# Front of a mixture-of-experts block: zero rows leave earlier, GpSimd normalises 20 of 32 tiles, the statistics and the router weights in another order

## Chip, cores and metric

One core of a Trainium2 chip runs the kernel. The metric is the device time of one execution in microseconds (us). The kernel before the change takes 130.73 us, the median of 3 runs (130.49 to 130.87).

## What is computed

The input x holds 16 sequences of 256 tokens, 128 wide: 4096 tokens. The result is x plus the outputs of two branches on the layer-normalised x. One branch is a gated recurrence, the other sends each token to one of 8 experts.

```python
xn = _layernorm(x, axis=-1)
x = x + _L0_attn_ref(xn, ...) + _L0_ffn_ref(xn, ...)

# recurrence: causal depthwise convolution of 4 taps, two gates, scan, projection, RMS norm
r_t = sigmoid(x_conv @ W_r.T + b_r);  i_t = sigmoid(x_conv @ W_i.T + b_i)
a_t = a_base ** (8.0 * r_t)
h = a * h + b                       # over the 256 tokens of a sequence
out = out @ W_out.T * rms * gamma

# experts: E = 8, capacity 512 tokens each
eidx = argmax(softmax(xf @ Wr))
rank = cumulative count of earlier tokens of the same expert;  keep = rank < cap
ye = relu(xf[dispatch] @ W1) @ W2
y  = zeros.at[dispatch].add(ye * probability)
```

## The kernel before

The 4096 tokens are 32 tiles of 128 tokens (NT = 32). They are loaded and normalised in five units, `UNITS = ((0, 4), (4, 4), (8, 8), (16, 8), (24, 8))`, first tile and count. Each of the five engines has one program, written out by hand in the order in which it runs, and engines wait for each other by semaphores. An engine that waits stops everything behind the wait in its program.

The front, which the change touches, runs from the start to the first gather of expert rows:

- SP (sync) issues the five loads of x (L314), then waits for the last of them (L315), then issues the weights of expert 0 (L318). It then issues, for each unit, the write of the normalised rows to the DRAM buffer `xn_rows` (L323) as soon as the unit is normalised, with the weights of expert 1 behind the third. Last come gamma (L326) and four writes of zeros to the result rows `y_rows` (L330).
- DVE takes mean and variance of a unit (`moments(u)`, L874), and after ACT's square root (`root(u)`, L682) the reciprocal and the offset (`inverse(u)`, L882 and L884). The offset releases the normalisation of the unit. It also routes: `marks(h)` (L918 to L934) finds the expert of each token of half h (16 tiles) and counts along a partition, `ranks(h)` (L943 to L947) adds the counts from PE, `places(h)` (L952 to L964) makes the masks `hi_val` and `low_eq`. At the end the table from PE is turned into `idx_in` and `idx_out` (L985, L986).
- POOL (GpSimd) builds constants, writes the numbers `values` (L385, four instructions), normalises its tiles (`POOL_TILES`, L380), and makes the four diagonal matrices of the convolution taps, `diag` (L396), between units 2 and 3. Later it issues the indirect gathers (L405) and scatters (L417).
- ACT evicts the transposed raw tiles (`untile(n)`, L694), normalises its tiles (`ACT_TILES`, L689) and evicts the transposed normalised tiles (`keep_columns(n)`, L698).
- PE starts with 7 matmuls on the identity whose result nobody reads (L442, two passes each). It transposes raw x (L507), makes the centred router weights (L513), computes router logits (L453), and counts over partitions (`counts(h)`, L461 to L473). The order on PE in the middle of the front is fixed by these lines:

```python
for n in range(1, 3):
    columns_of(n)          # L495, transposes of normalised tiles
conv(0, 0, 2)              # L537, L539; waits for diag_done = 4 (L524)
counts(1)                  # L461 to L473; waits for run of marks(1)
...
table_of(0)                # L481
columns_of(3)
conv(0, 2, 3)
table_of(1)                # L481; its result is read by idx_in
```

The first gather waits for all of `xn_rows` to have landed (`xn_out`, L424) and for `idx_in` (L426). After it PE transposes the gathered rows (`turn(0)`, L594) and the expert matmuls begin. POOL issues 64 gathers and scatters from there to the end of the expert stage, and PE has work in all of it.

Of the kernel before, what the change touches and what calls it, by code (L numbers as in the profile page):

```python
# [13 lines left out]
P = 128  # L14
# [4 lines left out]
C = 4  # L19
TC = T // C  # L20
# [26 lines left out]
def rglru_moe_kernel(nc, x, params, gamma, weights, xn_rows, y_rows, out):  # L47
# [3 lines left out]
    def tile_rows(dram, t0, nt):  # L51

        return dram[t0 * P:(t0 + nt) * P, :].rearrange("(g p i) d -> p g (i d)", p=P, i=RUN)

    def runs(buf, t0, nt):
        return buf[:, t0 * D:(t0 + nt) * D].rearrange("p (g w) -> p g w", w=RUN * D)

    def own_rows(dram, t0, nt):

        return dram[0:T, :].rearrange("(p t) d -> p t d", t=NT)[:, t0:t0 + nt, :]  # L60

    def tiles(buf, t0, nt):
        return buf[:, t0 * D:(t0 + nt) * D].rearrange("p (t d) -> p t d", d=D)

    with ExitStack() as ctx:
# [6 lines left out]
        def sem(name):  # L72
            return ctx.enter_context(nc.semaphore(name))
# [70 lines left out]
        zeros = sca[:, 0:TC]  # L144
# [33 lines left out]
        NU = len(UNITS)  # L178

        x_in = [sem(f"x_in{u}") for u in range(NU)]  # L180
# [3 lines left out]
        zeroed = sem("zeroed")  # L184
        zero_out = sem("zero_out")
# [81 lines left out]
        block = ctx.enter_context(nc.Block())  # L267


        POOL_TILES = (2, 3, 6, 7, 10, 11, 14, 15, 18, 19, 22, 23, 26, 27, 30)  # L270
        ACT_TILES = (0, 1, 4, 5, 8, 9, 12, 13, 16, 17, 20, 21, 24, 25, 28, 29, 31)

        COUNT_AT = 6
        PE_CONV = 2
# [1 line left out]
        def normalised(eng, n):  # L276
            for done, mine in ((norm_act, ACT_TILES), (norm_pool, POOL_TILES)):
                count = sum(t < 4 * (n + 1) for t in mine)
                if count:
                    eng.wait_ge(done, count)  # L280
# [30 lines left out]
        @block.sync  # L311
        def _(sp):
            for u, (t0, nt) in enumerate(UNITS):
                sp.dma_start(runs(x_tok, t0, nt), tile_rows(x_rows, t0, nt)).then_inc(x_in[u], 16)  # L314
            sp.wait_ge(x_in[NU - 1], 16)  # L315

            def first_weights(e):
                sp.dma_start(w_raw[:, e, :], weights[:, e * WW:(e + 1) * WW]).then_inc(w_in[e], 16)  # L318

            first_weights(0)  # L320
            for u, (t0, nt) in enumerate(UNITS):
                normalised(sp, (t0 + nt) // 4 - 1)
                sp.dma_start(own_rows(xn_rows, t0, nt), tiles(xn_tok, t0, nt)).then_inc(xn_out, 16)  # L323
                if u == 2:
                    first_weights(1)
            sp.dma_start(gam[:, :], gamma.partition_broadcast(P)).then_inc(gam_in, 16)  # L326

            sp.wait_ge(zeroed, 1)
            for c in range(C):
                sp.dma_start(y_rows[c * TC:(c + 1) * TC, :].rearrange("(p j) d -> p (j d)", p=P),  # L330
                             zeros).then_inc(zero_out, 16)

            for e in range(2, E):
                sp.wait_ge(gather_in[e - 2], 16 * ST)
                sp.dma_start(w_raw[:, e, :], weights[:, e * WW:(e + 1) * WW]).then_inc(w_in[e], 16)

            sp.wait_ge(scattered, 16 * NS)
            for n in range(NH):
                sp.dma_start(tiles(ybuf, 4 * n, 4), own_rows(y_rows, 4 * n, 4)).then_inc(y_in[n], 16)
            for n in range(0, NH, 2):  # L340
                sp.wait_ge(final_done, n + 1)
                sp.dma_start(tile_rows(out_rows, 4 * n, 4), runs(ybuf, 4 * n, 4)).then_inc(stored, 16)
            sp.wait_ge(stored, 16 * NH)

        @block.gpsimd
        def _(pool):
# [28 lines left out]
            def normalise(u):  # L375
                t0, nt = UNITS[u]
                pool.wait_ge(nmr_done, u + 1)
                for t in range(t0, t0 + nt):
                    if t in POOL_TILES:
                        g.tensor_scalar(xn_tok[:, t * D:(t + 1) * D], x_tok[:, t * D:(t + 1) * D], rstd[:, t:t + 1],  # L380
                                        nmr[:, t:t + 1], ALU.mult, ALU.add).then_inc(norm_pool, 1)
# [8 lines left out]
            normalise(0)  # L390
            normalise(1)
            normalise(2)
            pool.wait_ge(par_in, 16)
            pool.wait_ge(ident_done, 1)
            for k in range(TAPS):
                g.tensor_scalar(diag[:, k, :], ident[:, :], par[:, CONV_W + k:CONV_W + k + 1], 0.0, ALU.mult,  # L396
                                ALU.add).then_inc(diag_done, 1)
            normalise(3)
            normalise(4)

            def gather(e):
                if e > 0:
# [35 lines left out]
        def _(pe):  # L438
            mm = nc.tensor.matmul
            pe.wait_ge(ident_done, 1)  # L440
            for _ in range(7):
                mm(bank[7][:, 0:P], ident[:, :], ident[:, :], start=True, stop=True)  # L442


# [227 lines left out]
        def _(act):  # L672
# [4 lines left out]
            def root(u):  # L677
                t0, nt = UNITS[u]
                if u == 0:
                    act.wait_ge(eps_done, 3)  # L680
                act.wait_ge(stat_done, (t0 + nt) // 2)
                a(std[:, t0:t0 + nt], stats[:, t0:t0 + nt, 2], ACT.Sqrt, bias=eps[:, 0:1],  # L682
                  scale=1.0 / D).then_inc(std_done, 1)

            def normalise(n):
                act.wait_ge(nmr_done, 1 + next(u for u, (t0, nt) in enumerate(UNITS) if 4 * n < t0 + nt))
                for t in range(4 * n, 4 * n + 4):
                    if t in ACT_TILES:
                        a(xn_tok[:, t * D:(t + 1) * D], x_tok[:, t * D:(t + 1) * D], ACT.Identity,  # L689
                          scale=rstd[:, t:t + 1], bias=nmr[:, t:t + 1]).then_inc(norm_act, 1)  # L690

            def untile(n):
                act.wait_ge(tp_done, n + 1)
                a(xT[:, n * HT:(n + 1) * HT], tp[n % 2][:, :], ACT.Copy).then_inc(xT_act, 1)  # L694

            def keep_columns(n):
                act.wait_ge(xn_tp, n + 1)
                a(xnT[:, n * HT:(n + 1) * HT].rearrange("d (p i) -> d p i", i=RUN),  # L698
                  xn_bank[n % 3][:, :].rearrange("d (i p) -> d p i", i=RUN), ACT.Copy).then_inc(xnT_done, 1)
# [4 lines left out]
            root(1)  # L704
            normalise(0)
            untile(2)
            normalise(1)
            root(2)
            untile(3)
            normalise(2)  # L710
            untile(4)
            normalise(3)
            root(3)
            untile(5)
            untile(6)
            normalise(4)
            normalise(5)
            root(4)
            untile(7)
            keep_columns(0)  # L720
            normalise(6)
            normalise(7)
            for n in range(1, 4):
                keep_columns(n)

            def lead(e):
# [127 lines left out]
        def _(dve):  # L854
# [14 lines left out]
            def moments(u):  # L869
                t0, nt = UNITS[u]  # L870
                dve.wait_ge(x_in[u], 16)
                for t in range(t0, t0 + nt, 2):

                    v.bn_stats(stats[:, t:t + 2, :].rearrange("p t c -> p (t c)"),  # L874
                               x_tok[:, t * D:(t + 2) * D].rearrange("p (j d) -> p d j", j=2)
                               ).then_inc(stat_done, 1)

            def inverse(u):
                t0, nt = UNITS[u]
                cols = slice(t0, t0 + nt)  # L880
                dve.wait_ge(std_done, u + 1)
                v.reciprocal(rstd[:, cols], std[:, cols]).then_inc(rstd_done, 1)  # L882
                dve.wait_ge(rstd_done, u + 1)
                v.scalar_tensor_tensor(nmr[:, cols], stats[:, cols, 1], -1.0, rstd[:, cols], ALU.mult,  # L884
                                       ALU.mult).then_inc(nmr_done, 1)

            moments(0)
            dve.wait_ge(centre_mm, 1)
            v.tensor_copy(w_router[:, :], centred).then_inc(router_w, 1)
            moments(1)  # L890
            inverse(0)
            inverse(1)
            moments(2)
# [2 lines left out]
            v.tensor_scalar(half_b[:, :], par[:, BIAS_R:BIAS_I + 1], 0.5, None, ALU.mult).then_inc(coef, 1)  # L896
            inverse(2)
            moments(3)
            results = [0]

            def put(ins):
# [64 lines left out]
                                        ALU.is_equal).then_inc(low_done, 1)  # L966

            marks(0)
            inverse(3)
            moments(4)  # L970
            ranks(0)
            inverse(4)
            places(0)
            marks(1)
            ranks(1)
# [129 lines left out]
            def scaled_projection(_):  # L1105
                dve.wait_ge(gam_in, 16)
                v.tensor_tensor(wog[:, :], par[:, WO_T:WO_T + D], gam[:, :], ALU.mult).then_inc(wog_done, 1)
# [97 lines left out]
```

## Time and profile before

| | |
|---|---|
| time, median of 3 runs | 130.73 us |
| span of the profiled execution | 128.8 us |
| PE busy | 106.2 us (82%) |
| DVE busy | 101.8 us (79%) |
| ACT busy | 99.6 us (77%) |
| POOL busy | 84.6 us (66%) |
| chain that ended last, PE's share | 60% |
| moved by DMA | 19.27 MB |

The time of an execution is its span, from the first to the last instruction, and what lies around it: 130.73 less 128.8 is 1.9 us. The page cuts the span into 40 slices of 3.2 us and gives the busy share of each engine in tenths; for the clock, 9 stands for the full rate:

```profile
PE   3999999999799999999999997999997999700000
DVE  5398998999699999979614489999999975973690
ACT  3299792888589589789689999999999799823560
POOL 8987774078788787778777877888787878700000
PEclk9999999999999999999999999999999999998555
```

### The profile page before, as it was taken

The numbers are of one execution on the slowest core, as the hardware profiler recorded it, in microseconds if no ns is written. First come the engines' busy times: TensorE is split into PE (matmuls) and PEld (weight loads), VectorE is DVE, ScalarE is ACT, GpSimd is POOL, SyncE is SP. The second block draws the span as 40 slices with busy tenths as digits, with TensorE's granted clock in tenths as the row PEclk, the third lists the DMA queues.
The fourth block names the chain that finished last, engine by engine and source line by source line (L and its number), as shares of the span: only waits on it lengthen the run. The fifth ranks groups of instructions, "written<-read, shape, count | busy, mean of one in ns | idle before, by whom it ended". The sixth has DMA issues, their size and how long they took to land.

```text
span 128.8 us, 2229 instructions
## 1 busy us (share of the span) xinstructions
PE 106.2 (82%) x711; PEld 89.9 (70%) x711; DVE 101.8 (79%) x238; ACT 99.6 (77%) x219; POOL 84.6 (66%) x109
## 2 busy tenths in 40 slices
PE   3999999999799999999999997999997999700000
PEld 3999976672379779789879987898697899600000
DVE  5398998999699999979614489999999975973690
ACT  3299792888589589789689999999999799823560
POOL 8987774078788787778777877888787878700000
PEclk9999999999999999999999999999999999998555
DMA  2966964892456365312611711111110111149995
GB/s 85 383 247 173 405 244 173 318 380 66 103 169 181 80 209 139 118 53 56 209 41 41 219 51 41 61 37 41 52 57 25 60 43 61 41 108 302 325 372 215
DMA packets 8234, 19.27 MB, mean 150 GB/s; under 512 B 1689, under 2 KB 1945, under 8 KB 8224
## 3 DMA queue, kind: packets, MB, share of 16 engines
q1 hardware_dynamic: 5424, 13.70, 31.5%
q0 software_dynamic: 2080, 4.19, 11.2%
q10 hardware_dynamic: 720, 1.25, 2.6%
q8 instruction: 5, 0.08, 0.2%
q14 instruction: 5, 0.04, 0.1%
HBM read 10.82 MB, written 8.39 MB: 149 GB/s over the span
## 4 chain that ended last, share of the span: by engine, by line
PE 60%; DVE 9%; DMA 8%; ACT 8%; issue 5%; POOL 4%; POOLq 1%; SPq 1%; DVEq 0%; ACTq 0%
PE bank L624 17%; PE bank L609 6%; PE bank L611 6%; PE bank L610 6%; DMA dec<-y_rows 4%; PE bank L640 4%; PE bank L453 3%; PE bank L561 3%; PE bank L442 3%; POOL xn_tok L405 3%; DMA xn_tok<-xn_rows,idx_in 2%; ACT xc L796 2%; PE bank L594 2%; PE bank L563 2%; PE bank L562 2%
## 5 line engine op out<-in xcount | busy, mean ns | idle before, releaser
L405 POOL DMA_INDIRECT xn_tok<-xn_rows,idx_in x32 | 33.7, 1054 | 14.4 <-issue 9.4
L417 POOL DMA_INDIRECT y_rows<-xn_tok,idx_out x32 | 33.5, 1047 | 9.7 <-issue 9.1
L624 PE MATMUL bank<-w_raw,h_sb 128*128 128x128 f32 x256 | 29.9, 275 | 0.0
L624 PEld LDWEIGHTS bank<-w_raw,h_sb 128*128 128x128 f32 x256 | 29.2, 192 | 0.0
L786 ACT ACTIVATE h_sb<-bank 128x512 f32<-128x512 f32 x32 | 18.8, 598 | 2.5 <-PE bank L611 0.6
L609 PE MATMUL bank<-xg_hi,w_hi 128*128 128x512 f32 x32 | 13.2, 412 | 0.0
L611 PE MATMUL bank<-xg_hi,w_lo 128*128 128x512 f32 x32 | 12.6, 393 | 0.0
L610 PE MATMUL bank<-xg_lo,w_hi 128*128 128x512 f32 x32 | 12.5, 391 | 0.0
L1021 DVE SCALAR_TENSOR_TENSOR xc<-xnT,par,xc 128x1020 f32<-128x1020 f32 (+2 forms) x9 | 11.5, 1277 | 0.3
L640 PE MATMUL bank<-par,xc 128*128 128x128 f32 x64 | 8.8, 280 | 2.2 <-ACT xc L796 1.3
L1061 DVE TENSOR_TENSOR_SCAN xnT<-dec,bank 128x256 f32<-128x256 f32 x16 | 10.1, 674 | 0.3
L640 PEld LDWEIGHTS bank<-par,xc 128*128 128x128 f32 x64 | 8.0, 191 | 3.1 <-ACT xc L796 1.6
L805 ACT ACTIVATE sq<-bank 128x128 f32<-128x128 f32 x32 | 8.9, 277 | 1.0 <-PE bank L640 0.3
L836 ACT ACTIVATE dec<-dec,prob 128x128 f32<-128x128 f32 x16 | 5.1, 389 | 5.8 <-DMA dec<-y_rows 5.8
L380 POOL TENSOR_SCALAR xn_tok<-x_tok,rstd,nmr 128x128 f32<-128x128 f32 x15 | 7.7, 529 | 2.8 <-DVE nmr L884 2.8
L453 PE MATMUL bank<-w_router,dec 128*128 128x128 f32 x64 | 8.6, 278 | 0.4 <-ACT dec L694 0.3
L754 ACT ACTIVATE dec<-bank,half_b 128x512 f32<-128x512 f32 x8 | 5.5, 689 | 4.2 <-PE bank L563 3.2
L453 PEld LDWEIGHTS bank<-w_router,dec 128*128 128x128 f32 x64 | 7.8, 192 | 0.9 <-ACT dec L694 0.5
L1028 DVE TENSOR_TENSOR xg_lo<-bank,xg_hi 128x512 fp32r<-128x512 f32 x8 | 5.5, 688 | 3.5 <-ACT xg_hi L778 3.3
L796 ACT ACTIVATE xc<-xnT 128x512 f32<-128x512 f32 x8 | 8.2, 1105 | 0.0
L609 PEld LDWEIGHTS bank<-xg_hi,w_hi 128*128 128x128 f32 x32 | 6.0, 188 | 2.5 <-DVE xg_lo L1028 0.9
L1045 DVE SCALAR_TENSOR_TENSOR inp<-inp,xc 128x512 f32<-128x512 f32 x8 | 5.2, 689 | 2.9 <-ACT inp L754 2.9
(143 smaller groups left out, 243.2 us busy)
## 6 DMA issues: line engine op xcount, KB each, us to landing
w_raw<-in_weights SPq DMA_DIRECT2D x8, 512.0 KB, 3.9
y_rows<-sca SPq DMA_DIRECT2D x4, 512.0 KB, 5.9
dec<-y_rows SPq DMA_DIRECT2D x8, 256.0 KB, 5.7
x_tok<-in_x SPq DMA_DIRECT2D x3, 512.0 KB, 5.9
xn_rows<-xn_tok SPq DMA_DIRECT2D x3, 512.0 KB, 3.6
out<-dec SPq DMA_DIRECT2D x4, 256.0 KB, 3.1
out<-dec ACTq DMA_DIRECT2D x4, 256.0 KB, 2.9
x_tok<-in_x SPq DMA_DIRECT2D x2, 256.0 KB, 3.5
```

Source lines behind the costliest of these rows:

```text
L405: g.indirect_dma_start(gathered[:, s * D:(s + 1) * D], None, xn_rows, bass.IndirectOffsetOnAxis(ap=idx_in[:, s:s + 1], axis=0)).then_inc(g ...
L417: g.indirect_dma_start(y_rows, bass.IndirectOffsetOnAxis(ap=idx_out[:, s:s + 1], axis=0), gathered[:, s * D:(s + 1) * D], None, bounds_che ...
L453: last = mm((bank[6], bank[2])[t // PT][:, o:o + D], xT[:, t * P:(t + 1) * P], w_router[:, :], start=True, stop=True)
L609: mm(b, w_hi[:, e % 2, w], xg_hi[:, :], start=True, stop=False)
L610: mm(b, w_hi[:, e % 2, w], xg_lo[:, :], start=False, stop=False)
L611: mm(b, w_lo[:, e % 2, w], xg_hi[:, :], start=False, stop=True).then_inc(h_mm, 1)
L624: last = mm(tile_of(e, s), h_sb[:, k * CAP + s * P:k * CAP + (s + 1) * P], w_raw[:, e, F + k * D:F + (k + 1) * D], start=(k == 0), stop=(k ...
L640: last = mm(obank[n % 3][:, i * D:(i + 1) * D], ordered[:, t * P:(t + 1) * P], par[:, WO_T:WO_T + D], start=True, stop=True)
L786: a(h_sb[:, k * CAP:(k + 1) * CAP], hbank[n % 3][:, :], ACT.Relu).then_inc(h_done, 1)
L796: a(ordered[:, cols].rearrange("d (i p) -> d p i", i=RUN), hs[:, cols].rearrange("d (p i) -> d p i", i=RUN), ACT.Copy).then_inc(order_done, 1)
L1021: ins = v.scalar_tensor_tensor(dst[:, :, back:], src[:, :, 0:L - back], par[:, k:k + 1], dst[:, :, back:], ALU.mult, ALU.add)
L1061: last = v.tensor_tensor_scan(hs[:, o:o + L], dec[:, o:o + L], given[:, s * L:(s + 1) * L], 0.0, ALU.mult, ALU.add)
```

## The change

Six edits, all ahead of the first gather.

1. POOL normalises 20 tiles instead of 15 and ACT 12 instead of 17. In units 3 and 4 POOL now has six tiles each (before four and three).
2. SP issues the zeros earlier: the first quarter behind the loads of x, the second behind unit 1's write, the third behind unit 2's, the last behind unit 4's. The wait for the last load of x is gone. Expert 0's weights come behind the third quarter of zeros, expert 1's behind the last.
3. POOL makes `diag` after normalising units 3 and 4 instead of before them.
4. PE runs 5 instead of 7 matmuls at the start.
5. ACT takes each `root(u)` ahead of a normalisation instead of behind it, and evicts `keep_columns(0)` after its last normalisation.
6. DVE takes `moments(1)` ahead of the copy of the router weights, and `moments(4)` and `inverse(3)` ahead of `marks(0)`; `inverse(4)` comes ahead of `ranks(0)`.

```diff
-        POOL_TILES = (2, 3, 6, 7, 10, 11, 14, 15, 18, 19, 22, 23, 26, 27, 30)
-        ACT_TILES = (0, 1, 4, 5, 8, 9, 12, 13, 16, 17, 20, 21, 24, 25, 28, 29, 31)
+        POOL_TILES = (2, 3, 6, 7, 10, 11, 14, 15, 17, 18, 19, 21, 22, 23, 25, 26, 27, 29, 30, 31)
+        ACT_TILES = (0, 1, 4, 5, 8, 9, 12, 13, 16, 20, 24, 28)
...
-            sp.wait_ge(x_in[NU - 1], 16)
...
-            first_weights(0)
+            sp.wait_ge(zeroed, 1)
+            clear(0)
             for u, (t0, nt) in enumerate(UNITS):
                 normalised(sp, (t0 + nt) // 4 - 1)
                 sp.dma_start(own_rows(xn_rows, t0, nt), tiles(xn_tok, t0, nt)).then_inc(xn_out, 16)
+                if u == 1:
+                    clear(1)
                 if u == 2:
-                    first_weights(1)
+                    clear(2)
+                    first_weights(0)
+            clear(3)
+            first_weights(1)
             sp.dma_start(gam[:, :], gamma.partition_broadcast(P)).then_inc(gam_in, 16)
...
             normalise(0)
             normalise(1)
             normalise(2)
+            normalise(3)
+            normalise(4)
             pool.wait_ge(par_in, 16)
             pool.wait_ge(ident_done, 1)
             for k in range(TAPS):
                 g.tensor_scalar(diag[:, k, :], ident[:, :], par[:, CONV_W + k:CONV_W + k + 1], 0.0, ALU.mult,
                                 ALU.add).then_inc(diag_done, 1)
-            normalise(3)
-            normalise(4)
...
-            for _ in range(7):
+            for _ in range(5):
                 mm(bank[7][:, 0:P], ident[:, :], ident[:, :], start=True, stop=True)
...
             normalise(0)
             untile(2)
+            root(2)
             normalise(1)
-            root(2)
             untile(3)
+            root(3)
             normalise(2)
             untile(4)
+            root(4)
             normalise(3)
-            root(3)
             untile(5)
+            normalise(4)
             untile(6)
-            normalise(4)
             normalise(5)
-            root(4)
             untile(7)
-            keep_columns(0)
             normalise(6)
             normalise(7)
-            for n in range(1, 4):
+            for n in range(0, 4):
                 keep_columns(n)
...
             moments(0)
+            moments(1)
             dve.wait_ge(centre_mm, 1)
             v.tensor_copy(w_router[:, :], centred).then_inc(router_w, 1)
-            moments(1)
...
             moments(3)
+            moments(4)
+            inverse(3)
...
             marks(0)
-            inverse(3)
-            moments(4)
+            inverse(4)
             ranks(0)
-            inverse(4)
             places(0)
```

## Rows read from the trace of the kernel before

**Rows 1.** Chain of waits, 17 to 33 us: start, us, engine, tile, line
```profile
17.48 1.38 DVE low_eq L964 x2
...
20.71 0.23 PE bank L470
...
24.91 0.19 DVE idx_in L985
...
30.07 3.12 DMA xn_tok<-xn_rows,idx_in
```

**Rows 2.** Timeline of POOL: start us, us, line, operation, count, idle time before
```profile
7.57 1.74 POOL L380 TENSOR_SCALAR xn_tok<-x_tok,rstd,nmr 128x128 f32<-128x128 f32 x4
12.08 1.55 POOL L396 TENSOR_SCALAR diag<-ident,par 128x128 f32<-128x128 f32 x4
14.44 1.73 POOL L380 TENSOR_SCALAR xn_tok<-x_tok,rstd,nmr 128x128 f32<-128x128 f32 x4 [0.81 <-DVE nmr L884]
```

**Rows 3.** Timeline of POOL in short stretches, single instructions beside DVE's
```profile
12.77 0.47 POOL L396 TENSOR_SCALAR diag<-ident,par 128x128 f32<-128x128 f32 x1
17.11 1.22 POOL L380 TENSOR_SCALAR xn_tok<-x_tok,rstd,nmr 128x128 f32<-128x128 f32 x1 [0.94 <-DVE nmr L884]
18.31 0.88 POOL L380 TENSOR_SCALAR xn_tok<-x_tok,rstd,nmr 128x128 f32<-128x128 f32 x1
```

**Rows 4.** Timeline of PE around the first part of the convolution
```profile
18.61 1.02 PE L537 MATMUL bank<-xnT,diag 128*128 128x512 f32 x2
20.33 0.22 PE L461 MATMUL bank<-offset,ones 128*128 128x128 f16 x1
```

**Rows 5.** Timeline of DVE from inverse(2) to marks(1)
```profile
9.86 0.20 DVE L882 RECIPROCAL rstd<-std 128x8 f32<-128x8 f32 x1 [0.29 <-ACT std L682]
...
10.18 1.42 DVE L874 BATCH_NORM_STATS2 stats<-x_tok 128x6 f32<-128x256 f32 x4
11.83 0.29 DVE L918 TENSOR_REDUCE top<-bank 128x16 f32<-128x128 f32 x1 [0.23 <-PE bank L453]
12.48 0.59 DVE L922 TENSOR_TENSOR_SCAN nth<-emask,eq 128x128 f32<-128x128 f32 x1
13.94 0.19 DVE L882 RECIPROCAL rstd<-std 128x8 f32<-128x8 f32 x1
14.16 0.17 DVE L884 SCALAR_TENSOR_TENSOR nmr<-stats,rstd 128x8 f32<-128x8 f32 x1
14.25 1.42 DVE L874 BATCH_NORM_STATS2 stats<-x_tok 128x6 f32<-128x256 f32 x4
15.58 0.27 DVE L943 TENSOR_TENSOR picked<-bank,onehot 128x128 f32<-128x128 f32 x1
16.92 0.18 DVE L952 TENSOR_TENSOR in_block<-block_id,hi 128x64 f16<-128x64 f16 x1
18.79 0.28 DVE L918 TENSOR_REDUCE top<-bank 128x16 f32<-128x128 f32 x1
20.23 0.42 DVE L928 TENSOR_TENSOR_SCAN run<-tmask,onehot 128x128 f16<-128x128 f32 x1
```

**Rows 6.** Landing times of the five loads of x, then of the five xn_rows writes
```profile
DMA to landing us min/median/max: 3.4/4.9/6.7
...
DMA to landing us min/median/max: 3.4/3.9/4.7
```

**Rows 7.** Chain of waits at the start of PE
```profile
2.08 3.36 PE bank L442 x14
5.44 0.45 PE bank L507 x4
```

**Rows 8.** Busy time by stretch: us, PE, PEld, DVE, ACT, POOL, clock, DMA share, GB/s
```profile
31.00:33.20 2.20, 1.13 (x2) 0.30 (x2) 2.10 (x8) 1.42 (x3) 1.59 (x3) 1.00 0.14 45
118.00:119.00 1.00, 0.00 (x0) 0.00 (x0) 0.00 (x0) 0.91 (x4) 0.00 (x0) 0.50 1.09 264
```

**Rows 9.** DMA issues of the page: median us from issue to landing of the gathers
```profile
xn_tok<-xn_rows,idx_in POOLq DMA_INDIRECT x32, 2.8
```

More of the change, by code:

```diff
@@ L314, in _, with clear @@
                 sp.dma_start(runs(x_tok, t0, nt), tile_rows(x_rows, t0, nt)).then_inc(x_in[u], 16)
-            sp.wait_ge(x_in[NU - 1], 16)
             def first_weights(e):
                 sp.dma_start(w_raw[:, e, :], weights[:, e * WW:(e + 1) * WW]).then_inc(w_in[e], 16)
-            first_weights(0)
+            def clear(c):
+                sp.dma_start(y_rows[c * TC:(c + 1) * TC, :].rearrange("(p j) d -> p (j d)", p=P),
+                             zeros).then_inc(zero_out, 16)
+            sp.wait_ge(zeroed, 1)
+            clear(0)
             for u, (t0, nt) in enumerate(UNITS):
@@ L323, in _ @@
                 sp.dma_start(own_rows(xn_rows, t0, nt), tiles(xn_tok, t0, nt)).then_inc(xn_out, 16)
+                if u == 1:
+                    clear(1)
                 if u == 2:
-                    first_weights(1)
+                    clear(2)
+                    first_weights(0)
+            clear(3)
+            first_weights(1)
             sp.dma_start(gam[:, :], gamma.partition_broadcast(P)).then_inc(gam_in, 16)
[L328 to L331, printed above, removed]
             for e in range(2, E):
```

## Prediction, made before the changed kernel was run

> **What bounds the kernel now.** I read the chain of waits first, since busy shares (PE 82%, DVE 79%) say nothing of the front. Its stretch before the expert stage [rows 1] shows which work ends last: DVE's masks, then the counts on PE at 20.71 (L470), which waited for the scan of marks(1) that started at 20.23 [rows 5], then the table matmuls, then idx_in at 24.91. From there POOL issues four gathers; the last starts at 30.07 and lands 3.12 us later, and only then do the expert matmuls begin. Behind that PE is the chain and POOL has 64 gathers and scatters to issue, so what the front gains or loses by idx_in is gained or lost at the end, unless another wait of the front takes over. The change must be judged by when counts(1) runs. It stands in PE's program right behind conv(0, 0, 2), which ran from 18.61 to 20.33 [rows 4], was done in time, and found `diag` finished since 13.63 [rows 2]. That is the cover which the change removes. All times below are on the profiled execution's clock.
>
> **The start: 0.45 us gained.** PE's 14 warm-up passes took 3.36 us, 0.24 each; the four transposes behind them took 0.45, 0.11 each [rows 7]: the slow level of the clock, 1.2 GHz by the spacing, against 2.4. Four passes fewer save 0.96 us, but the transposes then run at the slow rate in their place, 0.96 instead of 0.45. Net 0.45. The first unit of x has landed by then: the shortest landing is 3.4 us behind an issue at 0.8 [rows 6]. Bounds: 0 (the slow stretch lasts longer by what was cut) to 0.96. PE, ACT's evictions and DVE's copy of the router weights move by about this. inverse(2) at 9.86 waited 0.29 for root(2), which now comes ahead of normalise(1); of that I take 0.2, between 0 and 0.29. So I put the statistics of unit 3 at 9.52 instead of 10.18 [rows 5]. The loads don't hinder: the last of x, issued at 2.7, lands after 6.7 us, at 9.4 [rows 6], and moments(4) wants it at 10.86.
>
> **DVE's new order: marks(1) 0.96 us earlier, if nothing else held it.** One unit of statistics takes 1.33 (14.25 to 15.58) and one inverse 0.31 (13.94 to 14.25) [rows 5]. So marks(0) starts at 9.52 + 2 x 1.33 + 0.31 = 12.49, instead of 11.83; marks(0) lasts 2.11 (11.83 to 13.94), inverse(4) 0.31, ranks(0) 1.03 (15.58 to the inverse's start, 16.92 less 0.31), so places(0) starts at 15.94 instead of 16.92, and marks(1), 1.87 later (16.92 to 18.79), at 17.8 instead of 18.79 [rows 5]. The offsets for POOL: unit 3's is ready at 12.4 (was 14.16), unit 4's at 14.8. The total of DVE's work is the same; the reordering only fills 0.23 us in which DVE waited for logits and brings the offsets forward. The scan of marks(1) starts 1.44 later, at 19.3, and is over at 19.7.
>
> **POOL: five tiles more, and diag behind all of them.** POOL starts 0.28 behind an offset (14.16 to 14.44 [rows 5, 2]), so unit 3 begins at 12.7. A tile costs 0.435 (1.74 for four [rows 2]); twelve tiles are 5.2 us. Some of unit 4's run beside places(0). There tiles took 1.22 and 0.88 us instead of 0.44 each while hi_val and low_eq ran on DVE, to 18.86 [rows 1, 3]: 1.2 us of loss for one passage of places. Unit 4 meets the same passage from 15.9 to 17.8, so I charge it once. POOL ends at 12.7 + 5.2 + 1.2 = 19.1 (it ended at 19.6 before, 18.31 + 0.88 + 0.44, so the normalisation alone would be no loss). Then come four diag, 1.55 [rows 2], and 0.1 for one beside a scan of marks(1) (0.47 instead of 0.39 before [rows 3]): diag is ready at 20.8, not 13.63.
>
> **PE: the wait that this makes.** conv(0, 0, 2) starts at 20.85 and takes 1.72 (18.61 to 20.33 [rows 4]), to 22.57. Queued behind it on PE are counts(1), the totals, both tables, columns_of(3) and the rest of the convolution. The counts' first two matmuls take 0.11, so L470 runs at 22.68 against 20.71 [rows 1]. Loss: **1.97 us**. The 0.96 us that DVE gained ends in a wait of DVE for before_done, some 3 us long (19.9, with `numbered` done, to 23.05). From L470 to idx_in everything is a sequence between PE and DVE in unchanged order: 24.91 + 1.97 = 26.9.
>
> **Edits with one answer, at nothing.** The zeros: four issues leave the stretch behind unit 4's write and come between the others. All four writes of xn_rows but unit 4's are early; unit 4 is normalised at 19.1, issued at 19.2, and lands after 3.4 to 4.7 us [rows 6], by 23.9, which is 3.0 before idx_in: the wait for xn_out costs nothing while the convolution is late, and without that cover it would be level with idx_in. The fourth gather landed in a stretch with the DMA engines at 0.14 [rows 8], so I take 0 for it; the median of all gathers is 2.8 [rows 9], so the bounds are 0 and -0.3. Both weights come later on SP, but are read behind the tables and have over 3 us. On ACT five tiles are taken away, 2.2 us; ACT isn't on the chain there [rows 1]. keep_columns(0) moves behind the last normalisation, still ahead of 18, and its cover is the same wait for diag. Three DMAs before the writes of xn_rows cost SP some tenths where it would wait for tiles.
>
> **Sum.** 130.73 + 1.97 = **132.7 us**. The profiled span of 128.8 with 1.9 around it is the median, so no correction. Bounds of the unknown terms: losing nothing to places (-1.2) and gaining the most at the start (-0.5) give 131.0, the quicker gather 130.7. Upwards, nothing gained at the start (+0.65) and the two scans of one marks, 0.59 and 0.42 [rows 5], blocking POOL (+1.0) give 134.3.
>
> **What a page would add.** Tiles beside places(0) lost 1.2 us, while the diag that ran beside the scan of marks(0), an instruction with two inputs in SBUF (0.59 us [rows 5]), lost 0.08 [rows 3]. The Trainium skill, SBUF — State Buffer, section Who interferes with whom, and the rule above it in SBUF: two separate sides, says that a VectorE instruction with two SBUF inputs and a GpSimd one that reads SBUF exclude each other for the whole instruction. Here the trace agrees for low_eq and hardly for the scan. By the page every such instruction would block POOL, by the rows only those of places.
>
> **Rivals.**
> 1. *The convolution isn't late* (the other side: faster). If diag were done by 18.95, conv would end by 20.68, level with before; if by 17.9, DVE's 0.96 would come through whole: 130.73 - 0.96 = 129.8. For it: DVE's and PE's orders do bring marks(1) forward. Against: from 12.7 twelve tiles and four diag without any loss take 5.2 + 1.55, to 19.45, already past the point. It needs tiles that start before DVE's offsets, so the sum must be wrong by 0.5 us at two places. Chance 0.09.
> 2. *Half of it*: diag at 18.95 to 19.3, by a start 0.9 earlier and little loss beside places, within 0.4 us of 130.73. Chance 0.07.
> 3. *Every DVE instruction with two SBUF inputs blocks POOL.* The two scans of a marks, 0.59 and 0.42 [rows 5], are 1.0, and POOL now works beside marks(0) and marks(1): 2.0 more at diag, 134.7. Against: the 0.08 of [rows 3]. Chance 0.05. This is the page's rule above, taken whole.
> 4. *PE's clock falls in the new wait*, which is some 2.2 us long (PE went from columns_of(2) into the convolution at 18.61 [rows 4] and now stands until 20.85). At the slow level conv(0, 0, 2) alone takes 1.7 us more, with transposes and the next part of the convolution 3: 134.4 to 135.7. Against: the clock was 1.00 in a stretch in which PE was busy 1.13 of 2.2 us, and at 118, some 4 us after PE's last matmul, it was 0.50 [rows 8]; a shorter gap than that isn't shown to drop it. Chance 0.06.
>
> **How the numbers follow.** The main case has 0.73, and its ends, 130.7 and 134.3, need several bounds to fall on one side at once. 131.2 to 134.0 holds nearly all of it and the upper edge of rival 2; outside lie rivals 1, 3 and 4, 0.20. A measurement can tell 0.3%, 0.4 us. Slower holds the main case and rivals 3 and 4, 0.84; within 0.3% rival 2, 0.07; faster rival 1, 0.09.
>
> **What would show it.** Right: in the after-profile diag (L396) runs from 19 to 21 behind twelve tiles; PE or its weight loads show a wait of 2 to 2.5 us released by POOL's diag L396 ahead of L537; DVE's L943 of ranks(1) waits about 3 us for PE; the chain of waits names POOL's L380 and L396 and then L537; idx_in at about 26.9; all behind it is shifted and alike. marks(0) at 12.5 and marks(1) at 17.8 to 18.5 show the part on DVE. Wrong: diag done before 19, or L537 released by something else, or idx_in before 25.2. If idx_in is late by 2 and the end isn't, the claim that the front passes through whole is wrong.

## Result: 133.93 us, slower; PE's wait for diag is the cause

The changed kernel takes 133.93 us, the median of 4 executions (132.48 to 134.82), beside 130.61 of the kernel before. The ratio is 1.0166 with an interval from 1.0101 to 1.0230; it leaves out two executions that lay more than 1.5% above the shortest. A second set gave 133.21 us and 1.0225 (1.0173 to 1.0276). The change costs 2.2 to 3.3 us.

The profiled execution is the shortest of the first set: 132.48 us, span 130.7. POOL is busier (86.8 us, before 84.6), ACT less (97.7, before 99.6), PE and DVE as before. The slices of 3.2 us, to be read against those of before:

```profile
PE   3989993999799999999999999899999799720000
DVE  5569795589979999979633469999999993993790
ACT  3278862079778869969959999999999799852660
POOL 8985999118787878787787787888777878710000
PEclk9999999999999999999999999999999999998555
```

ACT is all but idle in the eighth slice, from 22.9 to 26.1 us: it waits there for PE, which is busy in the whole of it. PE's own standstill lies before it, in the seventh slice. The chain of waits of the changed kernel (start, us, engine, tile, line) says what PE stood still for. It answers [rows 1]:

```profile
13.40 2.33 POOL xn_tok L384 x5
...
15.91 4.24 POOL xn_tok L384 x7
20.14 1.75 POOL diag L402 x4
...
21.94 1.12 PE bank L541 x2
...
24.04 0.06 PE bank L474
...
28.08 0.19 DVE idx_in L988
...
33.24 2.65 DMA xn_tok<-xn_rows,idx_in
```

Twelve tiles on POOL (GpSimd), then diag (now L402), then the first part of the convolution (L541), and only then counts(1) (L474, before L470). The list of waits of the changed kernel (who waited for whom: us in total, times, longest) shows PE waiting for diag, and DVE and ACT waiting for PE in turn:

```profile
ACT xnT L702 <- PE bank L499: 7.1, 3, 5.5
...
DVE picked L948 <- PE bank L579: 2.6, 1, 2.6
...
PE bank L541 <- POOL diag L402: 2.3, 1, 2.3
```

L474 runs at 24.04 where L470 ran at 20.71 [rows 1]; idx_in is at 28.08 instead of 24.91, 3.2 us later. The span is 1.9 us longer. Of the other 1.3, 0.5 is in the landing of the fourth gather (2.65 instead of 3.12 us, [rows 1]), the rest behind it. Behind the gathers nothing is given back in general: from the start of turn(0) on PE to the end of the span it was 95.5 us before (33.23 to 128.8) and 95.2 to 96.0 us in the profiles of all experiments from 2 to 12, whose turn(0) starts between 32.55 and 36.59. Only the two profiles of the changed kernel itself are shorter, 94.8 and 94.6; why is not known.

### The profile page after: what moved, and what is told of

It is laid out like the page before. It is cut to its first block, busy times and chain, and to the rows that moved or that the text cites. A ratio compares the mean times of both kernels' runs of the same rounds, so it can differ in the third digit from the quotient of the medians.

```text
span 130.7 us, 2221 instructions
## 1 busy us (share of the span) xinstructions
PE 106.7 (82%) x707; PEld 90.3 (69%) x707; DVE 102.2 (78%) x238; ACT 97.7 (75%) x214; POOL 86.8 (66%) x114
## 4 chain that ended last, share of the span: by engine, by line
PE 54%; DMA 12%; POOL 10%; ACT 8%; DVE 6%; issue 5%; SPq 2%; POOLq 1%; DVEq 0%; ACTq 0%
PE bank L628 16%; PE bank L613 6%; PE bank L615 6%; PE bank L614 6%; POOL xn_tok L384 5%; DMA x_tok<-in_x 5%; PE bank L644 4%; DMA dec<-y_rows 4%; DVE stats L877 3%; PE bank L565 3%; POOL xn_tok L409 2%; ACT xc L799 2%; PE bank L598 2%; PE bank L567 2%; PE bank L566 2%
## 5 line engine op out<-in xcount | busy, mean ns | idle before, releaser
L409 POOL DMA_INDIRECT xn_tok<-xn_rows,idx_in x32 | 33.2, 1038 | 15.3 <-issue 9.4
L384 POOL TENSOR_SCALAR xn_tok<-x_tok,rstd,nmr 128x128 f32<-128x128 f32 x20 | 10.2, 526 | 2.3 <-DVE nmr L887 2.3
L702 ACT ACTIVATE xnT<-bank 128x512 f32<-128x512 f32 x8 | 4.3, 600 | 7.1 <-PE bank L499 7.1
```

The source lines that it names most:

```text
L409: g.indirect_dma_start(gathered[:, s * D:(s + 1) * D], None, xn_rows, bass.IndirectOffsetOnAxis(ap=idx_in[:, s:s + 1], axis=0)).then_inc(g ...
```

## Experiments

Five questions: is it diag's place (theory A), is it the early zeros or the split (B), does PE's clock have a part (C), does the start of PE explain the size (D), and is there anything to gain. Times are medians, ratios are against the kernel before on the same chip. Experiments 1 to 4 ran on one chip, 5, 6, 7 and 9 on a second, 8 and 10 to 12 on a third, so across these groups the ratios are the fairer comparison.

**1. The changed kernel again.**

> The changed kernel as it is, once more, beside the kernel before. In the first set its executions spread from 132.5 to 134.8 us, with a mean granted clock of 0.958 in the shortest and 0.935 to 0.943 in the others. Theory A (PE waits 2.3 us for diag, and all else follows): a ratio of about 1.015, the waits as in the first profile. Theory C (in the new wait PE's clock falls in some executions, the fourth rival of the prediction): executions with a clock of 0.958 are about 132.5, those with less are 0.7 to 2.3 us longer.

Measured: 133.21 us (132.1 to 134.08), ratio 1.0225 (1.0173 to 1.0276), the same chain: diag until 21.5, idx_in at 27.64. Of the eight executions in both sets the three with a mean clock of 0.935 to 0.943 took 134.63, 133.23 and 134.82 us, the five with 0.947 and more 132.1 to 134.08, mean 133.0. None of the four executions of this set had a low mean clock, so it doesn't decide on C.

The mean clock of an execution is a blunt sign. It also holds the fall to 0.50 behind PE's last matmuls, which begins between 114 and 120 us in the traces: the profiled execution of experiment 4 has a mean of 0.948 and no low stretch in the front at all. Only a trace shows where the clock was low.

**2. Diag back in its place**, all else as changed.

```diff
             normalise(2)
-            normalise(3)
-            normalise(4)
             pool.wait_ge(par_in, 16)
...
                                 ALU.add).then_inc(diag_done, 1)
+            normalise(3)
+            normalise(4)
```

> The changed kernel with diag made before normalising units 3 and 4, as before the change. Theory A: PE has no wait for L541 longer than 0.3 us; L474 of counts(1) comes right behind the scan of marks(1), at 21.4 instead of 23.9; idx_in at about 25.6 instead of 28.1; time 2.5 us under the changed kernel, about 130.2, near the kernel before. Theory B (the early zeros and the tile split are the loss, the wait for diag only shows it): idx_in moves by less than 1 us. Theory C: the mean clock is 0.958 in every execution, since the 2.3 us wait is gone.

Measured: 130.13 us, ratio 0.9962 (0.9922 to 1.0003), 3.1 us under the changed kernel beside it. From its chain of waits:

```profile
21.35 0.06 PE bank L474
...
25.39 0.19 DVE idx_in L988
```

Counts(1) and idx_in come 2.2 to 2.7 us earlier. One edit of the six carries the whole loss; theory B falls. The split costs nothing by itself: with diag in front, POOL's last tile is done at 20.3, and the first gather still waits for DVE's L989 (idx_out) and not for the writes of xn_rows.

**3 and 4. Zeros back**, once with diag late, once with diag back. SP's front is that of before, the wait for x included.

> The changed kernel with SP's front as before the change: wait for all of x, expert 0's weights first, zeros last. Theory A with its correction (the first quarter of zeros, 512 KB written beside the loads of x, made the third load land at 8.1 instead of 6.6): statistics of unit 2 start at about 7.7 instead of 8.1, diag is ready 0.4 to 0.8 earlier than 21.9, and the time is 132.0 to 132.3 where the profiled run of the changed kernel had 132.5. Theory B: the time falls by over 1.5 us, to about the kernel before.

> Both undone: diag before units 3 and 4, SP's front as before. What is left of the change is the split 20 to 12, five warm-up matmuls and the order on DVE and ACT. Theory A: marks(1) starts at 18.3 to 18.8 (18.79 before the change), idx_in at 24.4 to 25.0, time 130.0 to 130.7, ratio to the kernel before 0.995 to 1.0. Theory B, by which the split is harmful in itself: over 131.3.

Measured: with diag late 133.76 us, ratio 1.0232 (1.0188 to 1.0277), idx_in at 27.97; with diag back 130.5 us, ratio 0.9996 (0.9968 to 1.0024), idx_in at 24.72. Putting the zeros back gains nothing in either pair. The expectation of 132.0 to 132.3 for the first was wrong. The third load of x landed at 6.2 instead of 8.1, but the statistics of unit 2 began at 8.06 all the same (8.12 in the first profile of the changed kernel), since the inverse of unit 1 waited for ACT's root, and ACT for PE's slow transposes.

**5. Diag late alone**, in the kernel before: the one edit of experiment 2, the other way round.

> The kernel before with one edit: diag is made after normalising units 3 and 4. Nothing else of the change. Theory A (the wait of PE for diag, and counts(1) queued behind it, is the loss): POOL is through its tiles at 19.6 and through diag at 21.2, conv(0, 0, 2) starts at 21.3 instead of 18.6, L470 of counts(1) comes at 23.1 instead of 20.7, and the time is 2.2 to 2.5 us over the kernel before, ratio 1.017 to 1.019. Theory B (the loss needs the split of the tiles or the early zeros): under 0.5 us.

Measured: 132.73 us (132.34 to 135.23), ratio 1.0122 (1.0060 to 1.0183). The edit alone makes the kernel slower, by 1.7 to 2.1 us in three executions with a clock of 0.954 to 0.957, a little under the 2.2 to 2.5 expected, and by 3.0 and 4.6 in two with 0.936 and 0.939. The profiled one is the first of these two. PE's wait in its timeline, then its chain of waits:

```profile
21.08 1.12 PE L537 MATMUL bank<-xnT,diag 128*128 128x512 f32 x2 [2.51 <-POOL diag L398]
```

```profile
19.40 1.63 POOL diag L398 x4
21.04 0.04 issue
21.08 1.12 PE bank L537 x2
22.20 1.34 PE bank L539 x2
...
23.75 0.11 PE bank L470
...
25.22 0.83 PE bank L495 x4
...
28.11 0.19 DVE idx_in L985
```

The second pair of convolution passes took 1.34 us (0.86 in the changed kernel's profile), four transposes 0.83 instead of 0.44. The busy time by stretch of the same trace, with the columns of [rows 8], shows why:

```profile
18.50:21.00 2.50, 0.07 (x1) 0.00 (x0) 2.10 (x7) 1.46 (x4) 2.50 (x6) 1.00 0.36 139
...
22.20:23.50 1.30, 1.30 (x5) 0.34 (x4) 0.00 (x0) 0.00 (x0) 0.17 (x1) 0.59 0.62 179
23.50:25.00 1.50, 1.50 (x24) 1.50 (x22) 0.85 (x3) 0.00 (x0) 0.00 (x0) 0.50 0.89 346
...
25.60:26.50 0.90, 0.90 (x5) 0.61 (x4) 0.90 (x3) 0.41 (x1) 0.00 (x0) 0.86 1.01 414
```

PE stood still for the 2.5 us ahead of diag's end and worked again from 21.08. The granted clock was still 1.00 to 22.4 and then 0.50, the 1.2 GHz level, to 25.8. The second convolution pair, the counts (0.11 us each instead of 0.06) and the four transposes took up to twice their time; the 16 matmuls of the first table took 1.14 us, as much as in the kernel before at the full clock. From the end of diag to idx_in it was 7.1 us here and 6.2 in five profiles with a late diag and the full clock (the changed kernel's two, experiments 3, 6 and 8): the low clock cost 0.9 us. The fourth rival of the prediction is real, at about half the smallest price it was given (1.7).

**6. Seven warm-up matmuls** in the changed kernel.

> The changed kernel with seven instead of five matmuls at PE's start. The term of 0.45 us in the prediction says that these two cost 0.45 us in the front: 0.3 to 0.5 us longer than the changed kernel (133.2). Theory D (how long PE runs at its slow rate at the start differs from execution to execution by over 1 us, whatever the number of warm-up matmuls): no difference beyond the spread, 132.8 to 134.0.

Measured: 134.48 us, ratio 1.0275 (1.0218 to 1.0333), idx_in at 28.72. That is 0.6 us later than in the first profile of the changed kernel. The time is over both expectations (0.3 to 0.5 us more, or 132.8 to 134.0): 1.3 us over experiment 1's median, in which low clocks are missing, and its two executions with a clock of 0.955 and more, 134.25 and 133.92, are 1.1 over the 133.0 of the changed kernel's like ones. The matmuls seem to cost something, but how much stays open: the intervals of the ratios overlap, and the slow stretch at PE's start, which wanders by itself (experiment 12), lasted here to about 8 us.

**7. The convolution behind counts(1).** Diag stays late. The whole of the convolution's first part moves behind the counts on PE.

```diff
             for n in range(1, 3):
                 columns_of(n)
-            conv(0, 0, 2)
             counts(1)
...
             columns_of(3)
-            conv(0, 2, 3)
+            conv(0, 0, 3)
```

> The changed kernel, with conv(0, 0, 2) moved on PE from ahead of counts(1) to the place of conv(0, 2, 3), behind columns_of(3). Diag stays late. Theory A, the part on the queue: what costs is not diag itself but that counts(1) stands behind its wait. Then ranks(1) starts at about 21.8 instead of 24.2 and waits under 0.5 us; the convolution's 1.7 us now stand ahead of table_of(1), whose masks are ready at 24.8, so idx_in comes 0.7 to 1.2 us earlier than in the changed kernel, about 27.0, and the time is 132.2. If it is no faster, the queue is not the place of the loss.

Measured in the profile, as expected: counts(1) waits for the scan of marks(1) and no longer for diag, and idx_in comes 0.8 to 1.3 us earlier. Timeline of PE, then the chain:

```profile
21.10 0.23 PE L474 MATMUL bank<-run,above 128*128 128x128 f16 x1 [1.67 <-DVE run L932]
...
26.81 0.19 DVE idx_in L987
```

The time doesn't follow: 133.42 us, ratio 1.0214 (1.0144 to 1.0283). Three of its four executions had a clock of 0.935 to 0.940; the one with 0.958, which is the profiled one, took 132.29 us, no less than the changed kernel's best (132.1). PE still stands still for 1.7 us. Up to turn(0) the gain is there (34.61 instead of 35.41 and 35.94); behind it this profile needs 95.4 us, as nearly all do, and the changed kernel's two 94.6 and 94.8. So the trace shows the queue behind the wait, and the time could not confirm what it is worth.

**8. The wait filled**: nine matmuls on the identity, which nobody reads, ahead of conv(0, 0, 2).

```diff
+            for _ in range(9):
+                mm(bank[3][:, 3 * P:4 * P], ident[:, :], ident[:, :], start=True, stop=True)
             conv(0, 0, 2)
```

> The changed kernel with nine more matmuls on the identity on PE between columns_of(2) and conv(0, 0, 2), 18 passes, some 2 us of work that nobody reads, in the place of the wait for diag. Theory C (in about half of the executions PE's clock falls to its half in or just behind that wait, as the trace of the kernel with diag late alone shows from 22 to 26 us, and this costs 1 us and more): no execution with a mean granted clock under 0.944, the wait for diag under 0.5 us, idx_in at 27.6 to 28.1 as in the first profile, and a time of 132.4 with less spread, against 133.2 to 133.9 of the changed kernel. If the clock has no part in the time: 133.2 to 133.9, as the changed kernel, with low clocks or without.

Measured: 132.72 us (132.19 to 133.42), ratio 1.0147 (1.0103 to 1.0191). The mean clock was 0.951 to 0.958 in all six executions. Timeline of PE, then the chain:

```profile
19.34 2.17 PE L577 MATMUL bank<-ident 128*128 128x128 f32 x18
21.82 1.12 PE L541 MATMUL bank<-xnT,diag 128*128 128x512 f32 x2 [0.31 <-POOL diag L402]
...
27.95 0.19 DVE idx_in L990
```

idx_in is as late as ever, and low mean clocks are absent. The median is 0.5 to 1.2 us under the changed kernel's, but the intervals of the ratios overlap (1.0103 to 1.0191, against 1.0101 to 1.0230 and 1.0173 to 1.0276), and the changed kernel never ran on this chip: that the filling makes it faster is likely and not shown. Its mean, 132.7, is near the 133.0 of the changed kernel's executions with a clock of 0.947 and more.

Over all runs, a mean clock of 0.943 or less was seen in 11 of 25 executions of the five kernels in which PE stands for 1.7 to 2.5 us in the front (the changed kernel in two sets, experiments 3, 5, 6 and 7), and in none of 88 executions of the others, the kernel before among them. The line was drawn afterwards, and the lowest of the 88 are at 0.944; but at 0.940 and less it is still 9 of 25 against none. With six executions of experiment 8 all at 0.951 and more this supports theory C as an addition to A. A fall of the clock in the front was seen itself in one trace only, experiment 5's; in the other ten executions it is inferred from the mean.

**9, 10 and 11. A version that beats both.** In experiment 2's chain PE waited 0.5 us for an eviction on ACT that stood behind root(3) and two tiles. Experiment 9 puts the evictions first, with diag back:

```diff
             untile(3)
-            root(3)
             normalise(2)
             untile(4)
-            root(4)
+            root(3)
             normalise(3)
             untile(5)
+            root(4)
             normalise(4)
```

> The changed kernel with diag back ahead of units 3 and 4, and on ACT root(3) behind untile(4) and root(4) behind untile(5). In the run with diag back alone the chain of waits runs from the statistics of unit 3 over ACT's root(3), two tiles and the eviction L698 to router L457 on PE at 13.16, then PE without a gap to counts(1). With the evictions ahead of the roots PE gets its tile 1 us earlier and waits for the scan of marks(0) only: counts(1) 0.3 to 0.5 us earlier, time 129.6 to 129.9, ratio 0.992 to 0.995. If marks(1)'s scan is then the later one, the gain is under 0.2.

> The changed kernel with diag back and ACT's roots behind the evictions, once more with more rounds, since its interval was wide (0.980 to 0.999). Theory A: every execution under the changed kernel's shortest of 132.1; median 129.8 to 130.2, ratio to before 0.992 to 0.996. Low clocks (under 0.944) are absent.

> The same with SP's front as before the change: zeros last. If the early zeros are worth something once diag is in its place, this is slower than the one beside it; from the runs so far (130.13 with zeros early and 130.5 with zeros late) 0.0 to 0.4 us: 130.0 to 130.5, ratio 0.994 to 0.999. If the write of 512 KB beside the loads of x costs anything at the end, it is faster instead.

Measured: 130.13 us, ratio 0.9897 with the wide interval 0.9800 to 0.9993, then in a larger set 129.75 us (128.96 to 130.34), ratio **0.9909 (0.9874 to 0.9944)**. It beats the kernel before by 0.9% and the changed one by 3.5 to 4.2 us. From the chain of the second:

```profile
21.04 0.06 PE bank L474
...
25.09 0.19 DVE idx_in L988
```

0.3 us ahead of experiment 2, as expected. With the zeros back at the end: 130.17 us, ratio 0.9951 (0.9924 to 0.9979). The early zeros seem to be worth 0.4 us: in all three pairs the kernel with them is the faster one, by 0.4 to 0.6 us, but in each the intervals overlap, so this isn't settled. It isn't gained at idx_in, which is at 25.04 with the zeros back and at 25.09 without.

**12. The kernel before again**, for its start.

> The kernel before, for a second look at its start. Theory D (the end of PE's slow stretch at the start wanders from execution to execution, with five warm-up matmuls and with seven): the end of the slow stretch lies somewhere between 5 and 8 us, not necessarily at 5.3 as in the first trace; idx_in moves with it, by up to 1 us. If it lies at 5.3 again, the first trace may show the rule for seven warm-up matmuls.

Measured: 131.59 us, span 129.5, idx_in at 26.00, 1.1 later than in the first profile of the same kernel. Timeline of PE, then the chain:

```profile
7.36 1.50 PE L453 MATMUL bank<-w_router,dec 128*128 128x128 f32 x8
...
26.00 0.19 DVE idx_in L985
```

The first router group took 1.50 us (1.13 in the first profile), the four transposes ahead of it 1.06 instead of 0.60: the slow stretch lasted to about 8 us, with seven warm-up matmuls. That it is slow is read from these durations; the granted clock of the profile stands at 1.00 from the start in every trace.

## Why the prediction was right, and where its sizes were off

- **The wait for diag (right in kind and place).** Predicted: diag at 20.8, PE waiting some 2.2 us, counts(1) queued behind it. Measured: diag at 21.9, a wait of 2.3 us, L474 behind it. Experiments 2 and 5 show it from both sides: taking that edit away gains 3.1 us, making it alone costs 1.2%.
- **The number (partly luck).** idx_in was predicted at 26.9 and came at 28.08 in the profiled execution, 1.2 late. The fourth gather landed 0.5 sooner and the rest was 0.7 shorter than was put down for them, so this execution took 132.5 us beside a forecast of 132.7. The errors behind idx_in, which the prediction had at nothing, made up for the one ahead of it.
- **POOL's sum, 1.1 us short.** Timeline of POOL, the changed kernel:

```profile
13.40 6.75 POOL L384 TENSOR_SCALAR xn_tok<-x_tok,rstd,nmr 128x128 f32<-128x128 f32 x12 [1.23 <-DVE nmr L887]
20.13 1.76 POOL L402 TENSOR_SCALAR diag<-ident,par 128x128 f32<-128x128 f32 x4
```

  The tiles began at 13.4 instead of 12.7 (0.7), took 6.75 instead of 6.4 (0.35), and diag 1.76 instead of 1.65 (0.1). The one passage beside places(0) was the right charge: the one tile that began at 18.07, beside hi_val and low_eq, took 1.65 us, 1.2 more than the others, and the two scans of marks(0) cost about 0.3 together. The third rival, by which every DVE instruction with two SBUF inputs blocks POOL for 2 us more, is out: the excess over 5.2 us was 1.5, and 1.8 with diag's, not 3.2.

  The hold-up also goes the other way. DVE's L952, with two SBUF inputs, took 0.39 us beside the tiles; its counterpart took 0.17 before, with POOL idle, and so did L952 itself later on, with POOL idle:

```profile
16.90 0.34 DVE L951 TENSOR_SCALAR hi<-rank 128x16 f16<-128x16 f32 x1
17.27 0.39 DVE L952 SCALAR_TENSOR_TENSOR lo<-rank,hi 128x16 f16<-128x16 f32 x1
...
25.22 0.17 DVE L952 SCALAR_TENSOR_TENSOR lo<-rank,hi 128x16 f16<-128x16 f32 x1
```

  The section Who interferes with whom of the Trainium skill's SBUF — State Buffer says that the order of issue decides which of the two engines blocks. By that rule L952 waits for a tile already running, and the trace agrees. But L951, which reads one tensor, took 0.34 instead of 0.17 as well, so two inputs alone don't explain it.
- **The start (term mis-sized).** I put the statistics of unit 3 at 9.52. They began at 10.25, after 10.18 before the change, so of the 0.66 us forecast nothing was gained; marks(1) began at 19.5 instead of 17.8. Timelines of PE and of DVE, the changed kernel:

```profile
5.66 1.06 PE L511 MATMUL bank<-ident,x_tok 128*128 128x128 f32 x4
6.51 1.31 PE L457 MATMUL bank<-w_router,dec 128*128 128x128 f32 x8
...
7.57 0.18 DVE L885 RECIPROCAL rstd<-std 128x4 f32<-128x4 f32 x1 [1.10 <-ACT std L686]
...
16.16 0.29 DVE L948 TENSOR_TENSOR picked<-bank,onehot 128x128 f32<-128x128 f32 x1 [0.50 <-PE bank L477]
```

  The second transposes ran at the slow rate too; in the one trace that I had, the slow stretch ended at 5.3, with the warm-up matmuls. DVE waited 1.1 us for ACT's root(1), queued behind the eviction of those transposes. I took one execution's end of the slow stretch for a constant; experiment 12 shows the kernel before with a later one. And ranks(0) waited 0.5 us for PE, which had waited for ACT's eviction behind root(3): an order that I had put down as a gain.
- **"The loads don't hinder" (wrong, without effect here).** The landing times of the five loads were these, against [rows 6]:

```profile
DMA to landing us min/median/max: 3.3/6.4/8.5
```

  The third load, 6.4 us behind its issue at 1.71, landed at 8.1 instead of 6.6, beside the first zeros. In the second profile of the changed kernel it took 4.8 us, and in the kernel before, which has no zeros there, 4.9 and 5.4, so this differs between executions and the zeros aren't shown to be its cause. The last load landed 8.5 us behind its issue, at 11.2 instead of 9.4, and still 0.4 ahead of moments(4), which the late start had moved back. Experiment 3 shows that it decided nothing.
- **The clock (the rival with 0.06).** By the mean clock it came in 11 of 25 executions. In the changed kernel the three of them took 134.2 us in the mean and the other five 133.0, an estimate of 1.2 us; experiment 5's trace has 0.9. I argued from a stretch in which PE was busy 1.13 of 2.2 us [rows 8]. That stretch didn't stand still for 2.3 us; it was no evidence for one that does. And 118 us is not some 4 us behind PE's last matmul, which was done at 112.6. The clock goes with the 133.93 of the first set, in which three of four executions had it low. It doesn't explain why the second set, with none, has 133.21 and not 132.7; the wandering start, up to 1.1 us at idx_in, is wide enough for that, and no run took it apart.
- **From idx_in to the end (right).** The shift passes through whole, by the 95.2 to 96.0 us that follow turn(0) in the profiles of all other kernels. In the changed kernel's own two it doesn't quite: 0.7 to 0.9 us came back there. The fourth gather, put at no change with -0.3 as its bound, landed 0.5 sooner.

## What to carry to other kernels

Before something is moved back on a slack engine, look at what the consumer has queued behind its wait: four instructions of 0.4 us on GpSimd, moved behind twelve tiles, held a count that did not need them. A wait of 2.5 us on PE cost more than its length in one trace, since the clock fell behind it; in the traces beside it, with waits of 2.3 us, it didn't. So one trace doesn't tell what such a wait costs. And when the offending edit is taken out, try the rest again: five of these six edits, with one order on ACT mended, made the kernel 0.9% faster.

## What the hardware did that I had not expected

- PE's clock fell to 0.50 behind a standstill of 2.51 us in one trace (experiment 5), 1.3 us after PE had begun to work again, and stayed at 1.00 behind one of 2.28 to 2.35 us in four others (the changed kernel's two, experiments 3 and 6). The mean clocks of the changed kernel, 0.935 to 0.958, suggest that it falls in some executions of one kernel and not in others; no kernel has a trace of both.
- The end of PE's slow stretch at the start lay between about 5.3 and 8 us in the traces: at 5.3 and 8 with seven warm-up matmuls, between about 5.5 and 7.6 with five. In two profiles of the kernel before it goes with 1.1 us at idx_in (24.91 and 26.00) and 0.7 us of span; how much of the spread between other executions is due to it is not shown.
- The fourth gather took 3.12 and 3.07 us to land in the kernel before and 2.55 to 2.70 in all eleven profiles with POOL's new split, with zeros early and late (2.65 in experiment 3); with the old split and diag late (experiment 5) it took 2.81. I have no explanation; no experiment took it apart.
